# Own buffers and an interleaved order for a dense head's attention, passes dealt anew over the slots, hit matrices two to a slot, adjacency cast in place

## Chip, cores and metric

The kernel runs on one NeuronCore of a Trainium2 chip. The metric is the device time of one execution in microseconds, the median of repeated runs. The kernel before takes 17072.46 us (three runs, 17061.4 to 17086.94).

## What is computed

Sixteen graphs of 512 nodes with 128 features pass one layer made of two residual blocks:

```python
def gnn(x, adj):                      # x is layer-normed
    a = adj.astype(x.dtype)
    h = einsum('bnf,fu->bnu', x, W_msg)
    messages = einsum('bij,biu->bju', a, h) / sum(a, axis=1)      # mean over neighbours
    return relu(x @ W_upd + messages + bias)

def ffn(x):                           # x is layer-normed; 8 heads, 128 wide
    q = (x @ Wq) * 128 ** -0.5
    sim = einsum('pbnhd,pkhd->pbnhk', x @ Wq_pk, pk_keys)         # 2 sides of 128 keys
    # the 16 best of each side, the 16 best sums of 256 pairs, softmax of these:
    kv_scores, indices = product_keys(sim)
    k = einsum('bnhk,bnhkd->bnhd', kv_scores, keys_table[indices])
    v = einsum('bnhk,bnhkd->bnhd', kv_scores, values_table[indices])
    attn = softmax(where(causal, einsum('bihd,bjhd->bhij', q, k), -max))
    return einsum('bhij,bjhd->bhid', attn, v).reshape(b, n, 1024) @ Wo

x = x + gnn(layernorm(x), adj)
x = x + ffn(layernorm(x))
```

Each head has a table of 16384 rows of 256 numbers (key and value).

## The kernel before

The program goes over 16 batches (graphs). `batch` is written out for the first and the last one and is the body of a loop for the 14 between. Every engine has its own program, in an order that is fixed by hand; the engines meet at semaphores, and an engine whose next instruction waits does nothing else.

Seven of the eight heads are **gathered**. A batch has 28 **slots**; slot n is tile t = n % 4 (128 tokens) of head h = n // 4. For each slot POOL issues 16 indirect DMAs of table rows into one of three buffers `got` (L343). They need the row numbers (`rows_ready`) and the end of the slot that last read the buffer (`combined`). Row numbers come two tiles at a time: VectorE ranks the next head's scores in the four slots of a head and, at the end of slots t = 1 and t = 3, makes `lifted`; TensorE's `move` turns it into `score_ps`, and VectorE writes `rows` and `spread`. TensorE weighs the gathered rows (`comb_ps`, L580), ScalarE copies them to `kv`, and a chain of small steps does the tile's attention: `key_transpose`, `scores`, VectorE's `negate`, ScalarE's `exponent`, `prob_transpose`, `values`, `project`, VectorE's `add`.

The eighth head is **dense**: its whole table streams through `tab` (1 MB a chunk, SP's queue), and 128 **passes** a batch multiply it with weights that are worked out for every key. A pass is `raise_` (ScalarE, `expo`), `weigh` (VectorE, `wide`, L1114), `turn` (TensorE, four transposes, L456), a copy on ScalarE (`wideT`), and `multiply` (TensorE, L470). VectorE is one pass ahead of TensorE and can't run farther ahead (`wideT_ready`). Each slot has five places for passes, between the steps of its attention; the tuples `ONE`, `SIX` and `FEW` say how many stand at each place, and `MIDDLE` and `ENDING` say which tuple a slot has. Before, slots 1, 2, 15 and 16 have two passes and all others five.

The dense head needs, per batch, eight **hit matrices**: VectorE writes one (`hit`, 16 instructions, L1078), TensorE adds its 16 parts up (`add_hits`, L437), and VectorE takes the sum. They stand one in each of the slots 3 to 6 and 23 to 26.

The dense head's own attention has four tiles per batch. Two are done in slots 15 and 16 and two in slots 1 and 2 of the following batch (`OWN`, `LEFT`), each after the slot's gathered tile, with the same tensors `neg`, `prob`, `probT`, `headT` and the same parts of `score_ps` and `probT_ps`.

`front` (the next head's scores and queries) runs on TensorE ahead of the combine of a slot with t = 0, so its time counts to the slot before. The graph block of the next batch is spread over slots 8 to 20; the adjacency matrix is loaded as integers into `adj_i` and cast by ScalarE into `adj_f`.

## Time and profile before

| what | value |
|---|---|
| median time | 17072.46 us |
| span of the profiled execution, first to last instruction | 9595.0 us |
| time of the profiled execution beside its span | not recorded: the profile gives the span alone |
| median time less the span | 7477.5 us |
| TensorE busy (matmul) | 8080.2 us, 84% |
| VectorE busy | 7220.8 us, 75% |
| ScalarE busy | 4866.4 us, 51% |
| POOL busy, not counting the time between two issues | 6794.0 us, 71% |
| mean granted TensorE clock | 0.888 of 2.4 GHz |

The span has all 16 batches in it (7168 gathers, 448 slots of 16). What the device does outside of it, 44% of the time, leaves no instruction in the trace. No engine is full, and the shares are averages over slots that differ. A slot is read from one group of gathered matmuls (L580) to the next.

### The profile page before, as it was taken

The numbers are of one execution on the slowest core, as the hardware profiler recorded it, in microseconds if no ns is written. First come the engines' busy times: TensorE is split into PE (matmuls) and PEld (weight loads), VectorE is DVE, ScalarE is ACT, GpSimd is POOL, SyncE is SP. The second block draws the span as 40 slices with busy tenths as digits, with TensorE's granted clock in tenths as the row PEclk, the third lists the DMA queues.
The fourth block names the chain that finished last, engine by engine and source line by source line (L and its number), as shares of the span: only waits on it lengthen the run. The fifth ranks groups of instructions, "written<-read, shape, count | busy, mean of one in ns | idle before, by whom it ended". The sixth has DMA issues, their size and how long they took to land.

```text
span 9595.0 us, 181229 instructions
## 1 busy us (share of the span) xinstructions
PE 8080.2 (84%) x51232; PEld 6240.2 (65%) x51232; DVE 7220.8 (75%) x32005; ACT 4866.4 (51%) x14163; POOL 6794.0 (71%) x7177
## 2 busy tenths in 40 slices
PE   5888888888888888888888888888888888888898
PEld 4666666666666766667666676666666666666676
DVE  7787777877777777777776777777777777877775
ACT  3555445455454554545445454454554545545454
POOL 5777767777677776777767777677776767767666
PEclk7899889998888998889888898898998989988898
DMA  4555445554454554545444454455554545545454
GB/s 126 166 171 161 155 154 162 163 162 158 155 160 158 162 165 150 160 157 166 158 152 158 159 164 157 155 162 161 164 165 150 166 151 165 167 150 160 146 167 138
DMA packets 445985, 1516.88 MB, mean 158 GB/s; under 512 B 123760, under 2 KB 141552, under 8 KB 379248
## 3 DMA queue, kind: packets, MB, share of 16 engines
q0 software_dynamic: 344064, 939.98, 32.5%
q1 hardware_dynamic: 100848, 564.37, 16.8%
q8 instruction: 456, 7.47, 0.3%
q14 instruction: 617, 5.05, 0.2%
HBM read 1499.66 MB, written 4.19 MB: 157 GB/s over the span
## 4 chain that ended last, share of the span: by engine, by line
PE 53%; DVE 36%; issue 5%; ACT 5%; DVEq 1%; DMA 0%; ACTq 0%; SPq 0%
PE dense_ps L470 20%; DVE wide L1114 10%; PE comb_ps L580 10%; PE wideT_ps L456 5%; PE front_ps L410 4%; DVE onehot L1005 4%; PE score_ps L446 4%; DVE chosen L1010 3%; DVE hits L1078 3%; DVE onehot L998 3%; PE score_ps L507 2%; PE score_ps L495 2%; PE probT_ps L513 2%; DVE neg L1131 1%; ACT expo L706 1%
## 5 line engine op out<-in xcount | busy, mean ns | idle before, releaser
L343 POOL DMA_INDIRECT got<-in_table,rows x7168 | 6792.1, 948 | 2778.2 <-issue 2203.5
L470 PE MATMUL dense_ps<-tab,wideT 128*128 128x256 f32 x16384 | 3959.9, 385 | 4.7 <-ACT kv_d L641 3.8
L470 PEld LDWEIGHTS dense_ps<-tab,wideT 128*128 128x128 f32 x16384 | 3002.5, 192 | 640.4 <-issue 274.7
L1114 DVE SCALAR_TENSOR_TENSOR wide<-const_ps,rank,expo 128x128 f32<-128x128 f32 x8192 | 2303.7, 344 | 1268.0 <-PE wideT_ps L456 993.1
L706 ACT ACTIVATE expo<-sim_d,shift 128x128 f32<-128x128 f32 x8192 | 2596.8, 393 | 118.0 <-DVE wide L1114 117.3
L641 ACT ACTIVATE wideT<-wideT_ps 128x512 f32<-128x512 f32 x2048 | 1212.0, 592 | 1070.2 <-PE wideT_ps L456 1065.8
L456 PE MATMUL wideT_ps<-ident,wide 128*128 128x128 f32 x8192 | 1237.1, 274 | 118.3 <-DVE wide L1114 61.0
L456 PEld LDWEIGHTS wideT_ps<-ident,wide 128*128 128x128 f32 x8192 | 1005.9, 141 | 386.0 <-DVE wide L1114 101.6
L580 PE MATMUL comb_ps<-got,spread 128*32 128x256 f32 x14336 | 1078.7, 452 | 4.8 <-DVEq L1102 4.0
L446 PE MATMUL score_ps<-group_of,lifted 128*128 128x16 f32 x1792 | 344.1, 329 | 554.3 <-DVE lifted L1021 554.3
L580 PEld LDWEIGHTS comb_ps<-got,spread 128*32 128x32 f32 x14336 | 481.5, 126 | 491.3 <-issue 299.5
L446 PEld LDWEIGHTS score_ps<-group_of,lifted 128*128 128x128 f32 x1792 | 327.2, 273 | 591.9 <-DVE lifted L1021 565.4
L641 ACT ACTIVATE kv<-comb_ps 128x256 f32<-128x256 f32 x448 | 170.8, 381 | 878.1 <-PE comb_ps L580 876.7
L1078 DVE TENSOR_SCALAR hits<-iota_f,top_f_d,put 128x128 bf16<-128x128 f32 x2048 | 579.3, 357 | 0.6 <-DVE z_inv L1089 0.2
L746 ACT ACTIVATE prob<-neg,neg_max 128x128 f32<-128x128 f32 (+3 forms) x512 | 286.7, 560 | 518.9 <-DVE neg_max L1131 515.8
L641 ACT ACTIVATE sim<-front_ps 128x512 f32<-128x512 f32 x224 | 133.8, 597 | 819.8 <-PE front_ps L410 816.8
L501 PE MATMUL probT_ps<-ident,prob 128*128 128x128 f32 x1280 | 257.8, 304 | 300.3 <-ACT prob L746 300.3
L513 PE MATMUL probT_ps<-wo_sb,headT 128*128 128x128 f32 x1024 | 288.3, 369 | 187.8 <-ACT headT L641 187.8
L501 PEld LDWEIGHTS probT_ps<-ident,prob 128*128 128x128 f32 x1280 | 165.9, 153 | 394.4 <-ACT prob L746 394.4
L641 ACT ACTIVATE headT<-score_ps 128x128 f32<-128x128 f32 x512 | 141.8, 277 | 532.9 <-PE score_ps L507 532.9
L1005 DVE TENSOR_TENSOR onehot<-onehot,const_ps 128x1600 f32<-128x1600 f32 (+1 forms) x225 | 406.4, 1806 | 1.2
L998 DVE TENSOR_TENSOR onehot<-place,const_ps 128x1600 f32<-128x1600 uint32 (+1 forms) x225 | 406.8, 1808 | 0.0
(155 smaller groups left out, 8417.1 us busy)
## 6 DMA issues: line engine op xcount, KB each, us to landing
tab<-in_dense SPq DMA_DIRECT2D x512, 1024.0 KB
got<-in_table,rows POOLq DMA_INDIRECT x7168, 2.7
adj_i<-in_adj SPq DMA_DIRECT2D x16, 1024.0 KB, 9.6
x_in<-in_x SPq DMA_DIRECT2D x16, 256.0 KB
out<-fin SPq DMA_DIRECT2D x16, 256.0 KB, 6.0
tab<-in_wqpk_t SPq DMA_DIRECT2D x1, 512.0 KB, 11.0
tab<-in_keys_t SPq DMA_DIRECT2D x1, 512.0 KB, 15.5
wq_sb<-in_wq SPq DMA_DIRECT2D x1, 512.0 KB, 15.2
```

What stands on the lines that cost most here:

```text
L343: pool.indirect_dma_start(out=got[got_no(n)][:, g, :], out_offset=None, in_=table, in_offset=bass.IndirectOffsetOnAxis(ap=rows[:, t * GATH ...
L446: mm = pe.matmul(moved_ps[:, 2 * q + u, :], lifted[:, u, q, :, :].rearrange("p e r -> p (e r)"), group_of[:, :], start=True, stop=True)
L456: mm = pe.transpose(wideT_ps[:, q * P:(q + 1) * P], wide[k % 2][:, q, :], ident[:, :])
L470: mm = pe.matmul(dense_ps[:, v * 2 * D:(v + 1) * 2 * D], wideT[k % 2][:, (2 * u + v) * P:(2 * u + v + 1) * P], tab[(k // CHUNK) % 2][:, (2 ...
L513: pe.matmul(proj_ps, headT[:, :], wo_sb[:, h, :], start=True, stop=True).then_inc(projected, 1)
L580: mm = pe.matmul(comb_ps[j * BAND:(j + 1) * BAND, 0:2 * D], spread[:, t, g, :], got[got_no(n)][:, g, :], start=(c == 0), stop=(c == PER_BA ...
L641: return act.activation(dst, src, ACT.Copy, scale=scale)
L706: last = act.activation(expo[k % 2][:, 2 * u + v, :], sim_d[:, 2 * half + v, 0:NKEYS], ACT.Exp, bias=shift1[:, 2 * half + v, key:key + 1])
L998: after(link(dve.tensor_tensor(onehot[:, 0:nt, :, :].rearrange("p t k c -> p (t k) c"), place[:, t0:t0 + nt, :].rearrange("p t k -> p (t k ...
L1005: after(link(dve.tensor_tensor(hot, hot, cand_row[:, 0:nt, :].unsqueeze(2).broadcast_to([P, nt, TOPK, NCAND]), ALU.mult)))
L1078: last = dve.tensor_scalar(hits[:, a, :], iota_f[:, :], top_f_d[:, u, side, a:a + 1], put[:, u, side, a:a + 1], ALU.is_equal, ALU.mult)
L1114: last = dve.scalar_tensor_tensor(wide[k % 2][:, 2 * u + v, :], count_ps[:, v, :], rank1[:, 2 * half + v, key:key + 1], expo[k % 2][:, 2 * ...
```

## The change

The passes are dealt as 3 to 6 (in the last batch 3 to 7) a slot. The first slot of a head mostly has six, the fourth three or four. `THREE` and `FOUR` have no pass between `key_transpose` and `scores`, and `THREE` has none between `prob_transpose` and `values`. The last batch ends its passes with slot 23.

The dense head's attention has tensors of its own (`neg_d` to `headT_d`), the two banks of `front_ps` and its own semaphores. Each of its steps stands right behind the same step of the slot's gathered tile. Its own two tiles move from slots 15 and 16 to 17 and 18.

The hit matrices are made two to a slot, with two buffers, in slots 4, 8, 24 and 26. The adjacency matrix is cast onto itself, and its next load waits for the messages instead of the cast. The dense query moves from slot 3 to 5, and the graph block's matmuls are one slot earlier. Nothing is computed that was not computed before.

```diff
-ONE = (1, 1, 1, 1, 1)
+THREE = (1, 0, 1, 1, 0)
+FOUR = (1, 0, 1, 1, 1)
+FIVE = (1, 1, 1, 1, 1)
 SIX = (2, 1, 1, 1, 1)
-FEW = (1, 1, 0, 0, 0)
+SEVEN = (2, 1, 1, 2, 1)
-MIDDLE = [ONE] + [FEW] * 2 + [ONE] * 12 + [FEW] * 2 + [ONE] * 11
+MIDDLE = [
+    FIVE, FOUR, FOUR, THREE,
+    SIX, FOUR, FIVE, THREE,
...
-OWN = {15: 0, 16: 1}
+OWN = {17: 0, 18: 1}
 LEFT = {1: 2, 2: 3}
-OWN_LAST = {15: 0, 16: 1, 25: 2, 26: 3}
+OWN_LAST = {17: 0, 18: 1, 25: 2, 26: 3}
+HITS = {1: {4: (0, 1), 8: (2, 3)}, 0: {24: (0, 1), 26: (2, 3)}}
...
-    adj_f = sb("adj_f", [P, T, N])
+    adj_f = adj_i[:, :, :].bitcast(F32)
...
+    score_d_ps = front_ps[0]
+    headT_d_ps = front_ps[0][:, 0:P]
+    probT_d_ps = front_ps[1]
...
-                sp.wait_ge(adj_cast, b + 1)
+                sp.wait_ge(msg_ready, b * 2 + 2)
...
+        def key_transpose_dense(c, tile, f):
+
+            pe.wait_ge(kv_d_copied, c - tile + (tile // 2 * 2 + 2))
+            pe.wait_ge(q_copied, f)
+            pe.wait_ge(sim_copied, f * 2)
+            pe.wait_ge(added_d, c)
+            pe.transpose(keyT_d_ps, kv_d[:, tile, 0:D], ident[:, :]).then_inc(keyT_d_ready, 1)
...
+                values(slot, t)
                 if tile is not None:
...
+                    values_dense(c, tile)
+                project(slot, h)
+                if tile is not None:
+                    project_dense(c)
...
+                for g in sets:
+                    take_sum(of_d, half, g, sets[-1])
```

On TensorE, in slot 1 of a middle batch, this stood there before (tensors whose names end in `_d` are the dense head's; its attention here uses the common `score_ps` and `probT_ps`):

```order
L491 MATMUL probT_ps<-ident,kv 128x128
L470 MATMUL dense_ps<-tab,wideT 128x256 x4
...
L495 MATMUL score_ps<-keyT,qT 128x256
L501 MATMUL probT_ps<-ident,prob 128x128 x2
L507 MATMUL score_ps<-probT,kv 128x128 x2
L513 MATMUL probT_ps<-wo_sb,headT 128x128
...
L491 MATMUL probT_ps<-ident,kv_d 128x128
...
L495 MATMUL score_ps<-keyT_d,qT_d 128x384
L501 MATMUL probT_ps<-ident,prob 128x128 x3
L507 MATMUL score_ps<-probT,kv_d 128x128 x3
```

In the same slot of the changed kernel the order is this:

```order
L541 MATMUL probT_ps<-ident,kv 128x128
...
L571 MATMUL front_ps<-ident,kv_d 128x128
L545 MATMUL score_ps<-keyT,qT 128x256
...
L575 MATMUL front_ps<-keyT_d,qT_d 128x384
L520 MATMUL dense_ps<-tab,wideT 128x256 x4
...
L551 MATMUL probT_ps<-ident,prob 128x128 x2
L581 MATMUL front_ps<-ident,prob_d 128x128 x3
L520 MATMUL dense_ps<-tab,wideT 128x256 x4
...
L557 MATMUL score_ps<-probT,kv 128x128 x2
L587 MATMUL front_ps<-probT_d,kv_d 128x128 x3
L563 MATMUL probT_ps<-wo_sb,headT 128x128
```

Passes of the dense head now stand between the steps of both tiles, where before the second tile's steps followed one another with nothing between them.

On VectorE, in slot 4 of a middle batch, this stood there before (`wide` is a pass, `top_v` and `top_i` belong to the ranking):

```order
L1114 SCALAR_TENSOR_TENSOR wide<-const_ps,rank,expo 128x128 x4
L1078 TENSOR_SCALAR hits<-iota_f,top_f_d,put 128x128 x4
...
L939 MAX top_v<-sim 128x8 x4
L941 MAX_INDEX top_i<-top_v,sim 128x8 x4
...
L1114 SCALAR_TENSOR_TENSOR wide<-const_ps,rank,expo 128x128 x4
L1078 TENSOR_SCALAR hits<-iota_f,top_f_d,put 128x128 x4
L943 MATCH_REPLACE sim_rest<-top_v,sim 128x128 x4
```

In the changed kernel the same stretch reads so:

```order
L1211 SCALAR_TENSOR_TENSOR wide<-const_ps,rank,expo 128x128 x4
...
L1175 TENSOR_SCALAR hits<-iota_f,top_f_d,put 128x128 x4
...
L1034 MAX top_v<-sim 128x8 x4
L1036 MAX_INDEX top_i<-top_v,sim 128x8 x4
...
L1211 SCALAR_TENSOR_TENSOR wide<-const_ps,rank,expo 128x128 x4
L1175 TENSOR_SCALAR hits<-iota_f,top_f_d,put 128x128 x8
L1038 MATCH_REPLACE sim_rest<-top_v,sim 128x128 x4
```

The slot holds twice the hit instructions, and slots 3, 5, 6, 23 and 25 hold none.

## Rows read from the trace of the kernel before

**Rows 1.** Waits of POOL, whole run: total us, times, longest

```profile
POOL got L343 <- DVE rows L1029: 541.6, 123, 41.1
POOL got L343 <- PE comb_ps L580: 33.1, 20, 14.7
```

**Rows 2.** Timeline of POOL, first, middle, last: start, us, idle before

```profile
43.65 1.10 POOL L343 DMA_INDIRECT got<-in_table,rows  x1 [41.14 <-DVE rows L1029]
...
4800.49 0.95 POOL L343 DMA_INDIRECT got<-in_table,rows  x1 [0.30 <-issue]
...
9571.83 0.95 POOL L343 DMA_INDIRECT got<-in_table,rows  x1 [0.30 <-issue]
```

**Rows 3.** Windows: first, middle fourteen, last batch: us; busy PE PEld DVE ACT POOL; clock

```profile
115.90:675.96 560.06, 486.28 (x3154) 377.29 (x3153) 446.92 (x1988) 299.26 (x872) 410.23 (x433) 0.91 0.51 163
675.96:9000.60 8324.64, 7055.69 (x44801) 5452.17 (x44801) 6312.89 (x27960) 4256.78 (x12390) 5943.68 (x6274) 0.89 0.50 159
9000.60:9595.00 594.40, 501.86 (x3092) 381.60 (x3091) 381.89 (x1664) 293.26 (x867) 392.19 (x415) 0.88 0.47 148
```

**Rows 4.** Windows of one middle batch: its slots 1, 4, 5, 7, 8, 9, 11, 15, 23

```profile
4260.94:4287.97 27.03, 16.36 (x90) 11.54 (x90) 17.31 (x80) 8.38 (x27) 15.26 (x17) 0.69 0.38 123
...
4343.70:4359.29 15.59, 15.06 (x118) 12.49 (x118) 11.40 (x56) 11.25 (x35) 11.63 (x14) 1.00 0.51 161
4359.29:4382.88 23.59, 18.00 (x127) 14.68 (x127) 20.76 (x83) 11.55 (x36) 16.76 (x18) 0.95 0.50 157
...
4401.48:4425.43 23.95, 21.11 (x128) 16.35 (x128) 20.52 (x83) 11.54 (x34) 17.95 (x19) 0.93 0.59 193
4425.43:4439.84 14.41, 14.04 (x102) 11.53 (x101) 8.82 (x49) 10.92 (x34) 11.05 (x12) 1.00 0.47 141
4439.84:4458.98 19.14, 15.84 (x112) 12.90 (x111) 16.10 (x65) 14.11 (x40) 14.47 (x16) 1.00 0.57 190
...
4476.15:4499.41 23.26, 21.22 (x132) 16.24 (x132) 20.28 (x81) 12.14 (x35) 17.47 (x20) 0.94 0.60 196
...
4557.52:4589.18 31.66, 21.12 (x101) 14.84 (x100) 21.94 (x89) 7.91 (x24) 22.82 (x25) 0.68 0.43 134
...
4728.84:4757.10 28.26, 23.40 (x144) 18.11 (x143) 25.30 (x99) 11.77 (x34) 19.27 (x21) 0.88 0.46 141
```

**Rows 5.** Windows of the last batch: its slots 7 and 8

```profile
9172.91:9200.27 27.36, 25.11 (x140) 19.40 (x140) 19.86 (x76) 13.18 (x39) 17.25 (x19) 0.88 0.45 151
9200.27:9217.02 16.75, 16.38 (x113) 13.43 (x112) 10.38 (x55) 12.84 (x39) 12.79 (x14) 1.00 0.57 173
```

**Rows 6.** Waits of TensorE in that middle batch (4245.92 to 4843.14)

```profile
PE score_ps L446 <- DVE lifted L1021: 33.0, 12, 4.1
PE probT_ps L501 <- ACT prob L746: 18.8, 8, 5.7
PE probT_ps L513 <- ACT headT L641: 11.7, 32, 0.4
PE probT_ps L491 <- DVEq L1148: 7.1, 4, 4.3
PE score_ps L507 <- ACT probT L641: 4.2, 8, 0.7
```

**Rows 7.** Timeline of TensorE, slot 1 of that batch

```profile
4265.08 0.27 PE L491 MATMUL probT_ps<-ident,kv 128*128 128x128 f32 x1
...
4278.20 0.45 PE L491 MATMUL probT_ps<-ident,kv_d 128*128 128x128 f32 x1 [4.32 <-DVEq L1148]
```

**Rows 8.** Timeline of VectorE, slot 4 of that batch

```profile
4348.10 1.13 DVE L1114 SCALAR_TENSOR_TENSOR wide<-const_ps,rank,expo 128x128 f32<-128x128 f32 x4 [3.68 <-PE wideT_ps L456]
```

**Rows 9.** Waits of POOL in the first 660 us

```profile
POOL got L343 <- DVE rows L1029: 56.9, 8, 41.1
POOL got L343 <- PE comb_ps L580: 15.7, 2, 14.7
```

**Rows 10.** The cast of the adjacency: duration min/median/max in ns

```profile
L641 ACT ACTIVATE adj_f<-adj_i x16: 1899/1902/1909, 12.9 to 8666.7; 128x2048 f32<-128x2048 int32 x16
```

More of the change, by code:

```diff
@@ L81, in got_back, with dense_tile, fronts @@
     return next(d for d in range(1, 6) if got_no((n - d) % SLOTS) == got_no(n))
-def attend_no(b, n, left, first, last):
-    dense = set(OWN_LAST if last else OWN) | (set() if first else set(LEFT))
-    place = n + len([m for m in dense if m < n]) + left
-    return place if first else b * (SLOTS + T) + (place - 2)
+def dense_tile(b, n, first, last):
+    if n in (OWN_LAST if last else OWN):
+        return (OWN_LAST if last else OWN)[n], b
+    if n in LEFT and not first:
+        return LEFT[n], b - 1
+    return None, b
+def fronts(b, n, last):
+    return b * GH + (min(n // T + 2, GH) if last else n // T + 2)
 def program(nc, x, adj, w_msg, w_upd, bias, wqpk_t, keys_t, wq, table, dense, wo, out):
@@ L550, in batch @@
                     if h < GH - 1:
-                        front(b, h + 1, last)
+                        front(b, h + 1, first, last)
                     elif not last:
@@ L806, in batch @@
                 copy(kv[:, t, :], comb_ps[:, 0:2 * D]).then_inc(kv_copied, 1)
+                if n == 12 and not last:
+                    gnn_hu(b + 1)
                 k = passes(b, k, w[1], first, last)
-                take_keyT(a, t, keyT)
+                take_keyT(slot, t)
+                if tile is not None:
+                    take_keyT_dense(c, tile)
                 if n == 9 and not last:
@@ L814, in batch @@
                     gnn_adj(b + 1)
-                if n == 13 and not last:
-                    gnn_hu(b + 1)
                 if n == 17 and not last:
@@ L1197, in batch @@
                     half, of_d, o = 0, b + 1, n - PREP[0]
+                sets = HITS[1].get(n, ()) if half == 1 else HITS[0].get(n, ()) if half == 0 else ()
                 def hit_part(part):
-                    if half is not None and 3 <= o <= 6:
-                        hit(of_d, half, o - 3, part)
-                a = attend_no(b, n, 0, first, last)
+                    for g in sets:
+                        hit(of_d, half, g, part)
+                tile, of = dense_tile(b, n, first, last)
+                c = of * 4 + (tile or 0)
                 k = passes(b, k, w[0], last)
@@ L1227, in batch @@
                     gnn_in(b + 1)
-                if n == 15 and not last:
+                if n == 14 and not last:
                     gnn_msg(b + 1)
```

229 lines of the change are left out of this document (150 added, 79 removed).

## The prediction

> **What bounds the kernel now.** I read the waits of POOL first, because POOL looks idle for 29% of the span and is not. One gather takes 0.95 us and the next one starts 0.30 us behind it [rows 2]. From the first gather at 43.65 to the last at 9571.83 there are 7167 steps. Less the waits in between, 574.7 - 41.1 = 533.6 us [rows 1], that is (9528.2 - 533.6) / 7167 = 1.255 us a gather, 20.1 us a slot, and 562.2 us a batch of 28 slots. A middle batch takes 8324.64 / 14 = 594.6 us [rows 3]. So the gathers alone would need 95% of the time, and POOL can be handed 32 us a batch back at the very most.
>
> The other 32 us are POOL's waits for row numbers. Those come out of a loop between TensorE and VectorE, and that loop sets the pace of a middle batch. In the windows of one middle batch the reader is to see two kinds of slot. In slot 4 TensorE is busy for 15.06 of 15.59 us: TensorE is the limit. In slot 5 it is busy for 18.00 of 23.59 us and VectorE for 20.76: VectorE is the limit, and TensorE waits ahead of `move` [rows 4]. Over the batch the waits of TensorE name the two stalls: 33.0 us for `lifted` at the end of odd slots, and the steps of the dense tile's attention [rows 6]. Slots 1 and 15, which have only two passes, still last 27.0 and 31.7 us, at a granted clock of 0.69 and 0.68 [rows 4]; slots 2 and 16 are of the same kind.
>
> I therefore cost two chains per batch, the TensorE-VectorE loop (594.6 now) and the gathers (562.2, unchanged), and ask which is longer afterwards.
>
> **The dense tile's attention, four tiles a batch.** It stands alone in its slots, so each wait between its steps is bare. Going are 18.8 us ahead of the probabilities' transposes, 7.1 ahead of the key's transpose, 4.2 ahead of the values, and four of the 32 waits ahead of the projection, 4 x 0.37 [rows 6]: together 31.6 us. The 7.1 are the shared buffers: the dense tile can't begin before the gathered tile is added. Behind those waits `move` is queued, and POOL waits for its rows. The steps' own time stays, since the same matmuls are done. A stall can return if no pass covers it; slots 1, 17 and 18 have a pass or two between each pair of steps except key and scores. Bounds: 24.5 go if the 7.1 stay because VectorE is late for its own reasons in slot 1 (17.31 busy of 27.03), 31.6 go at best. I take 31.6.
>
> **The clock in these slots.** One transpose takes 0.27 us in slot 1 while the clock is up and 0.45 us behind the 4.32 us wait [rows 7], 1.6 times as long. At a mean of 0.68, 64% of slot 15 is at 1.2 GHz, the lower of the two levels, so of its 21.12 us of TensorE work 0.64 x 21.12 x (1 - 1/1.6) = 5.1 us are lost, and by the same sum 3.8 in slot 1. With slots 2 and 16 some 16 us a batch at most. The passes that move into these slots are then done at the higher clock, but slots 1 and 15 wait for VectorE as well. Bounds 0 and 16, I take 6.
>
> **Hit matrices.** A slot with one costs more than its like without one: slot 5 against slot 9 is 23.59 - 19.14 = 4.45, slot 23 against 11 is 5.0, slot 4 against 8 is 1.2 [rows 4]. They are dear where VectorE is the limit. Leaving are slots 3 and 23 (5.0 each), 5 and 25 (4.45 each), and 6 (I take the 1.2 of slot 4): 20.1 us. Coming are a first one in slot 8 (1.2) and a second one in 4, 8, 24 and 26. VectorE has a gap of 3.68 us in slot 4, waiting for TensorE's front and combine [rows 8], and the second matrix lies partly in it; each costs between 1.2 and 4.45. Coming in all: 6.0 to 19.0. Net -14.1 to -1.1, I take -8.
>
> **Passes.** They stay 128. By the new plan the first slots of the seven heads have 41 (32 before), the second 31 (32), the third 33 (32), the fourth 23 (32). Nine passes go from fourth slots to first ones. The last batch has one pass more per slot than a middle one at slots 7 and 8, which prices a pass: 27.36 - 23.95 = 3.4 in a fourth slot, 16.75 - 14.41 = 2.3 in a first [rows 4, 5]. By these rows the move gives 9 x (2.3 - 3.4) = -9.9. If instead VectorE alone holds the fourth slot, taking a pass away gives back just its 1.13 us there [rows 8], and the move costs 9 x (2.3 - 1.13) = +10.5. Between ends of both signs I take 0.
>
> **Holes.** Where a tuple has no pass between two steps, TensorE waits for ScalarE's copy, 0.4 us as ahead of the projection, 11.7 / 32 [rows 6]. Thirteen slots lack the second place, and five of them the fifth as well: 18 x 0.4 = +7. It is 0 if `lifted` is late anyway, since TensorE then waits the same time twice over. I take 7.
>
> **Edits at nothing.** The cast is one instruction of 1.9 us a batch in either form [rows 10]. Its next load now waits for messages of slot 13 of the batch before, long past when SP comes to it; without that cover SP's queue would hold up the table's chunks. The dense query and the graph block's matmuls move by a slot or two with the same instructions. The new waits on `added_d` in `front` are for tiles two or more slots back. The extra buffers cost nothing.
>
> **Sum.** Loop: 594.6 - 31.6 - 6 - 8 + 0 + 7 = 556.0 us a batch. Gathers: 562.2. They have come within about 1% of each other, and neither is even, so they will trip over each other now and then: rows come in pairs, POOL is at most three buffers ahead, and TensorE now meets gathers that have not landed. The first batch is such a case already: without left dense tiles it takes 560.1 us [rows 3], and POOL waits 72.6 - 41.1 = 31.5 us in it [rows 9], most of it in its start-up. I add 5 us to the longer chain: 567 a batch. That is 27.6 us less in each of 14 middle batches (386), 25 in the last one, which has the same stalls, and 0 in the first. In all 411 of the 502 us that POOL waits behind the first 660 us (574.7 - 72.6) [rows 1, 9]. Span 9595.0 - 411 = 9184.
>
> The median is 17072.5, 7477.5 above the span, and the trace has nothing of that part. I take it as unchanged: same inputs, same outputs. **17072.5 - 411 = 16,661 us.**
>
> **Rivals.**
>
> *The gathers become the only bound* (0.20). If the low ends hold, the loop falls to 594.6 - 31.6 - 16 - 14.1 - 9.9 = 523, TensorE waits for gathers in every slot, and all 502 us go: 16,570 us. For it: the first batch's 560 with two dense tiles still serial. Against it: 523 needs four low ends at once.
>
> *Half of it is given back* (0.20). With the high ends, 594.6 - 24.5 - 0 - 1.1 + 10.5 + 7 = 586.5, the loop stays the bound, and the change gives 8.1 x 15 = 122, 16,950 us. Midway between 556 and 586.5 it is 571, and the change gives 23.6 x 14 = 330, 16,740 us. The case is what lies between. For it: fourth slots where VectorE is busy for 20.3 of 23.3 us (slot 11). Against it: the price of a pass in slot 7.
>
> *Nothing comes of it* (0.05): the dense steps wait for each other in the new order too, since ScalarE and VectorE take both tiles in turn; 17,040 to 17,100.
>
> *The clock falls, and it is slower* (0.07). Stalls that were collected in four slots are now holes in all of them, beside waits for gathers, and TensorE is granted less everywhere. The mean in a middle batch is 0.89 [rows 3]; if all slots went to the 0.69 of slot 1, the half-speed share would go from 0.22 to 0.62, and 504 us of TensorE work would grow by about 0.40 x 504 x 0.375 = 76 us, to a loop of 556 + 76 = 632: 37.4 x 15 = 561 us slower, 17,630 us. It decides from a mean of about 0.79, where the growth eats the 38.6 us that the loop gained. Against it: slots 4 and 8, with the densest TensorE work, stand at 1.00, and passes are put into the starved slots. The Trainium skill ("TensorE: Matmul & The Clock Gate", The HAM clock gate) says that the default is the throttled state and that activity releases it. By that rule more and shorter waits speak against this change; the trace agrees so far that the clock is low where TensorE sits idle (0.69 at 16.36 busy of 27.03).
>
> **How the numbers follow.** The forecast (16,600 to 16,740) has 0.48. A measurement here tells changes from 0.2% on, 34 us. Faster than that: 0.48 + 0.20 + 0.19 of the third case = 0.87; same 0.05; slower 0.08 (the clock 0.07, the rest 0.01). The range runs from the gathers' floor with some room, 16,550, to 16,890, which takes in the better half of the third case and leaves out about 0.18.
>
> **What the profile will show.** Right: POOL's waits for rows fall from 541.6 to below 200 us; a middle batch takes 562 to 570; slots 1, 2, 17, 18 last about 20 to 22 us at a clock above 0.85; the waits ahead of the dense tile's transposes are gone; waits of `comb_ps` for gathers appear. The hit slots 4, 8, 24, 26 last 18 to 22 us, and slots 5 and 25 under 20. Wrong: a middle batch above 580 us with `lifted` as TensorE's largest wait and more than 33 us of it; a clock below 0.85; a gather step above 1.26 us; or a span that falls while the time does not, which would mean that the part outside the span is not fixed.

## The result, and the profile after

The changed kernel takes 16523.39 us (median of four runs, 16515.62 to 16534.99), and beside it the kernel before takes 17066.93 (four runs, 17061.18 to 17086.94). The ratio is 0.968, with a 95% interval of 0.9666 to 0.9694: 543.5 us less, where 411 were forecast. The time lies 27 us below the range.

The span of the profiled execution is 16533.2 us, 1.8 us below its own time of 16534.99. So almost nothing lies outside the span. The prediction had 7477.5 us there, worked out from a span and the times of other executions, and took them as fixed. The trace of before that is shown ahead comes from an execution in which signals between engines came on time; in every other traced execution of before or after with all its gathers back to back they came late.

From the page of the kernel after, its span, its engines and the chain that ended last:

```profile
span 16533.2 us, 180655 instructions
## 1 busy us (share of the span) xinstructions
PE 8989.4 (54%) x51232; PEld 6835.3 (41%) x51232; DVE 7249.1 (44%) x32005; ACT 4856.2 (29%) x14163; POOL 6787.8 (41%) x7177
...
another core or an unknown queue 40%; DVE 22%; PE 21%; issue 10%; ACT 6%; DVEq 0%; ACTq 0%; DMA 0%; SPq 0%
```

No engine is busy for more than 54%, and 40% of the chain has no releaser in this trace, on a kernel with one core. Windows of its first batch, its middle fourteen and its last one (span of the window, busy time of each engine, clock, DMA share, GB/s), to set against [rows 3]:

```profile
147.21:1160.28 1013.07, 548.09 (x3154) 417.99 (x3153) 449.91 (x1993) 298.73 (x872) 412.20 (x436) 0.74 0.28 90
1160.28:15563.28 14403.00, 7875.30 (x44802) 5986.98 (x44801) 6339.16 (x27972) 4248.27 (x12390) 5937.58 (x6272) 0.75 0.29 92
15563.28:16533.18 969.90, 530.27 (x3092) 401.80 (x3091) 379.71 (x1652) 292.11 (x867) 390.40 (x413) 0.75 0.29 91
```

A middle batch lasts 14403.00 / 14 = 1028.8 us. The busy time of VectorE, ScalarE and POOL is what it was in [rows 3]; the engines do the same work and stand still for longer. Windows of slots 1 to 6 of one middle batch, against [rows 4]:

```profile
7385.96:7406.82 20.86, 16.73 (x115) 13.54 (x114) 18.89 (x86) 11.36 (x37) 0.00 (x0) 0.95 0.15 51
7406.82:7462.41 55.59, 22.88 (x113) 16.09 (x112) 15.33 (x80) 9.73 (x29) 30.26 (x32) 0.65 0.30 95
7462.41:7485.89 23.48, 19.07 (x104) 13.82 (x103) 17.39 (x67) 8.12 (x24) 2.18 (x3) 0.80 0.21 63
7485.89:7540.08 54.19, 25.64 (x147) 19.23 (x146) 19.82 (x90) 12.29 (x37) 28.05 (x30) 0.68 0.36 114
7540.08:7556.39 16.31, 13.75 (x101) 11.10 (x100) 14.70 (x60) 10.74 (x33) 0.00 (x0) 1.00 0.19 67
7556.39:7608.53 52.14, 19.64 (x107) 15.25 (x106) 12.20 (x57) 9.40 (x28) 30.26 (x32) 0.67 0.33 101
```

The reader is to see that slots take turns. Where POOL issues 30 or 32 gathers, which are the gathers of two slots in one go, the slot lasts 52 to 56 us. Where it issues none to three, it lasts 16 to 23 us, as in [rows 4]. This goes on up to slot 23; slots 24 to 27 share out their gathers and last 32 to 37 us each in the mean of the middle batches. The waits of POOL over the whole run, against [rows 1]:

```profile
POOL got L388 <- DVE rows L1124: 6681.7, 210, 44.5
POOL got L388 <- issue: 2349.5, 6879, 30.1
POOL got L388 <- PE comb_ps L661: 585.2, 31, 32.0
```

POOL waits twelve times as long for `rows` as in [rows 1]. These are not the stalls of before: gathers and loop take turns. The largest waits of the other engines (total us, times, longest) say why:

```profile
DVE wide L1211 <- remote: 6089.0, 464, 42.4
PEld wideT_ps L506 <- issue: 6003.2, 676, 34.1
ACT wideT L722 <- remote: 5165.6, 403, 37.2
PE wideT_ps L506 <- ACT wideT L722: 3395.7, 315, 33.8
```

"remote" is a wait whose end the trace can put down to none of this core's engines, since the instruction waited for had long been done. One of them, step by step. First TensorE in one slot, 8004.81 to 8059.64:

```profile
8014.50 1.89 PE L520 MATMUL dense_ps<-tab,wideT 128*128 128x256 f32 x8
8024.28 1.09 PE L506 MATMUL wideT_ps<-ident,wide 128*128 128x128 f32 x4 [7.89 <-issue]
8025.16 3.62 PE L520 MATMUL dense_ps<-tab,wideT 128*128 128x256 f32 x8
8052.35 1.09 PE L506 MATMUL wideT_ps<-ident,wide 128*128 128x128 f32 x4 [23.57 <-ACT wideT L722]
```

ScalarE and VectorE in the same stretch:

```profile
8023.54 0.60 ACT L722 ACTIVATE wideT<-wideT_ps 128x512 f32<-128x512 f32 x1 [9.62 <-remote]
...
8051.61 0.60 ACT L722 ACTIVATE wideT<-wideT_ps 128x512 f32<-128x512 f32 x1 [18.40 <-remote]
```

```profile
8023.61 1.13 DVE L1211 SCALAR_TENSOR_TENSOR wide<-const_ps,rank,expo 128x128 f32<-128x128 f32 x4 [10.54 <-remote]
...
8051.69 1.13 DVE L1211 SCALAR_TENSOR_TENSOR wide<-const_ps,rank,expo 128x128 f32<-128x128 f32 x4 [16.26 <-remote]
```

And POOL:

```profile
8045.34 0.95 POOL L388 DMA_INDIRECT got<-in_table,rows  x1 [0.30 <-issue]
8078.50 0.94 POOL L388 DMA_INDIRECT got<-in_table,rows  x1 [32.21 <-DVE rows L1124]
```

POOL gathers in steps of 1.25 us up to 8045.34. While it does, TensorE's four transposes of 8024.28 end at 8025.4, and ScalarE, which copies what they made and has been idle for 18.40 us, starts at 8051.61, 26 us later and 5 us behind the end of POOL's last gather. TensorE then waits for that copy, VectorE for TensorE. POOL is silent until 8078.50, and the next slot, from 8059.64 on, goes at its normal pace (25.16 us). The trace also records when each signal takes effect. The listing has the median distance from the end of an instruction to the next recorded signal on its semaphore ("gathering" is an instruction that starts less than 1.6 us behind the start of a gather). Some signals are missing from the records, 93 of `dense_ps`'s 2048 in after, so medians are read and not the longest ones:

```
                                  POOL silent    POOL gathering
after, TensorE's dense_ps           0.014 us         9.4 us
after, TensorE's wideT_ps           0.014 us        10.6 us
after, ScalarE's wideT              0.009 us        13.0 us
before, the trace shown ahead,
        TensorE's dense_ps             -             0.014 us
```

So signals of TensorE and ScalarE arrive some 10 us late while POOL issues gathers back to back. VectorE's `wide` is on time in the median in the same stretches (0.011 us).

The Trainium skill ("Perfetto Trace Analysis", Summary: the profiler window per engine type) lists the propagation of a semaphore as hidden from the profiled windows of TensorE, VectorE and ScalarE. This trace agrees: VectorE and ScalarE are busy for 7249.1 and 4856.2 us, against 7220.8 and 4866.4 in the trace shown ahead, and the lateness shows only in idle time and, here, in the events of the semaphores. (TensorE is busy for 8989.4 us instead of 8080.2, at a granted clock of 0.745 instead of 0.888.)

The Trainium skill ("Perfetto Trace Analysis", Identifying the Most-Contended Engine) also judges VectorE, ScalarE and GpSimd (POOL) by occupancy, the share of time in which they execute, and says to optimize the engine with the highest first; of TensorE it takes the share of the peak arithmetic rate and the busy share of the weight loads instead. By the busy shares VectorE would come first here (44%), and POOL, whose gathers the next section shows to be the cause, stands at 41%, no higher than the weight loads.

### The profile page after: what moved, and what is told of

The parts are those of the page before. It is cut to its first block, busy times and chain, and to the rows that moved or that the text cites. A ratio compares the mean times of both kernels' runs of the same rounds, so it can differ in the third digit from the quotient of the medians.

```text
span 16533.2 us, 180655 instructions
## 1 busy us (share of the span) xinstructions
PE 8989.4 (54%) x51232; PEld 6835.3 (41%) x51232; DVE 7249.1 (44%) x32005; ACT 4856.2 (29%) x14163; POOL 6787.8 (41%) x7177
## 4 chain that ended last, share of the span: by engine, by line
another core or an unknown queue 40%; DVE 22%; PE 21%; issue 10%; ACT 6%; DVEq 0%; ACTq 0%; DMA 0%; SPq 0%
PE dense_ps L520 8%; DVE wide L1211 6%; PE comb_ps L661 3%; ACT expo L787 3%; PE wideT_ps L506 2%; DVE hits L1175 2%; DVE onehot L1100 2%; PE score_ps L496 2%; DVE onehot L1093 2%; DVE chosen L1105 1%; PE front_ps L460 1%; ACT wideT L722 1%; PE score_ps L557 1%; DVE lifted L1116 1%
## 5 line engine op out<-in xcount | busy, mean ns | idle before, releaser
L388 POOL DMA_INDIRECT got<-in_table,rows x7168 | 6785.8, 947 | 9720.1 <-DVE rows L1124 6681.7
L506 PE MATMUL wideT_ps<-ident,wide 128*128 128x128 f32 x8192 | 1477.8, 310 | 5993.1 <-ACT wideT L722 3395.7
L520 PE MATMUL dense_ps<-tab,wideT 128*128 128x256 f32 x16384 | 4572.7, 427 | 115.9 <-issue 99.4
L520 PEld LDWEIGHTS dense_ps<-tab,wideT 128*128 128x128 f32 x16384 | 3423.6, 219 | 935.6 <-issue 413.0
L545 PE MATMUL score_ps<-keyT,qT 128*128 128x512 f32 (+3 forms) x896 | 390.3, 523 | 244.3 <-issue 144.9
L557 PE MATMUL score_ps<-probT,kv 128*128 128x128 f32 x2240 | 366.2, 299 | 207.3 <-ACT probT L722 197.1
L722 ACT ACTIVATE probT<-probT_ps 128x128 f32<-128x128 f32 x448 | 194.4, 434 | 926.7 <-remote 689.5
L827 ACT ACTIVATE prob<-neg,neg_max 128x128 f32<-128x128 f32 x448 | 251.0, 560 | 696.2 <-DVE neg_max L1228 452.8
L1248 DVE SCALAR_TENSOR_TENSOR acc<-probT_ps,prob_inv,acc 128x128 f32<-128x128 f32 x414 | 145.3, 351 | 661.0 <-PE probT_ps L563 614.2
L557 PEld LDWEIGHTS score_ps<-probT,kv 128*128 128x128 f32 x2240 | 316.7, 210 | 227.0 <-ACT probT L722 215.9
L1105 DVE TENSOR_REDUCE chosen<-onehot 128x32 f32<-128x1600 f32 (+1 forms) x225 | 406.1, 1805 | 2.8
```

The lines of the kernel that those rows point to most:

```text
L388: pool.indirect_dma_start(out=got[got_no(n)][:, g, :], out_offset=None, in_=table, in_offset=bass.IndirectOffsetOnAxis(ap=rows[:, t * GATH ...
L506: mm = pe.transpose(wideT_ps[:, q * P:(q + 1) * P], wide[k % 2][:, q, :], ident[:, :])
L520: mm = pe.matmul(dense_ps[:, v * 2 * D:(v + 1) * 2 * D], wideT[k % 2][:, (2 * u + v) * P:(2 * u + v + 1) * P], tab[(k // CHUNK) % 2][:, (2 ...
L557: last = pe.matmul(headT_ps, kv[:, j, D:2 * D], probT[:, j * P:(j + 1) * P], start=(j == 0), stop=(j == t))
L722: return act.activation(dst, src, ACT.Copy, scale=scale)
L1105: link(dve.tensor_reduce(chosen[:, 0:nt, 0, :], onehot[:, 0:nt, :, :], AX.X, ALU.add))
```

## The experiments

Times differ from chip to chip and, on one chip, from one hour to another: the kernel before took 17067 us beside the changed kernel, and 17231, 17098, 17275, 17251, 17224 and 17259 us beside the kernels of this section, in their order; 17275 and 17224 are of one chip. So differences of tens of us are taken within one group, and across groups by the ratio to before.

**Two theories.** A: the time is in the span, the loop is slowed by late signals, and the trace shown ahead lacked them. B, the prediction's: something fixed lies outside the span. The first kernel is before, unchanged.

> The kernel before, unchanged, for a second trace. The changed kernel's trace has a span as long as its time (16,533 us), and in it signals of TensorE and ScalarE reach their waiters 10 us late in the median while POOL issues gathers, and 0.01 us late when it does not. The first trace of the kernel before had none of that and a span 7,477 us short of its median. Theory A (that trace caught an execution in a rare undisturbed condition; the timed ones have late signals too): the new span is 17,050 to 17,090 us, slots last about 20 us without gathers and 45 us or more with them, and a middle batch takes about 1,060 us. Theory B (the kernel's executions really span 9,600 us and some 7,470 us lie outside the instructions): the new span is 9,590 to 9,600 us again.

Its time is 17236.39 us and its span 17234.6. From the page, the middle fourteen batches, and the waits of POOL:

```profile
span 17234.6 us, 181229 instructions
...
PE 9315.1 (54%) x51232; PEld 6957.4 (40%) x51232; DVE 7244.2 (42%) x32005; ACT 4886.6 (28%) x14163; POOL 6781.2 (39%) x7177
```

```profile
1180.63:16195.62 15014.99, 8148.41 (x44801) 6085.19 (x44801) 6333.35 (x27965) 4275.29 (x12390) 5930.84 (x6271) 0.72 0.29 88
```

```profile
POOL got L343 <- DVE rows L1029: 7344.9, 209, 49.4
POOL got L343 <- issue: 2386.7, 6860, 34.3
POOL got L343 <- PE comb_ps L580: 536.7, 32, 33.4
```

B is gone: in every execution of before or after whose span is on record, timed or traced, span and time are less than 2 us apart. Of the trace shown ahead the own time isn't on record, so its 9595.0 us stood beside the times of other executions. A middle batch of before takes 15014.99 / 14 = 1072.5 us, not 594.6, and its waits for `rows` are 7344.9 us, not the 541.6 of [rows 1]. Signals are late here too: 6.7 us for `dense_ps` and 10.0 for `wideT_ps` and `wideT` in the median, measured as above.

**Are the gathers the cause?** Before and after with one gather a slot; the other fifteen are left out, and zeros stand in their place:

```diff
+KEEP = (0,)
...
-                for c in range(PER_BAND):
-                    for g in range(c, GATHERS, PER_BAND):
+                for g in KEEP:
```

> The kernel before with one gather a slot instead of 16; the other 15 parts of got hold zeros, so the attention of the seven gathered heads is computed from wrong keys and values with the same instructions. Theory (gathers hold back the signals of the other engines): the late signals are gone, and the span is that of the TensorE-VectorE loop alone, 594.6 us a middle batch as in the undisturbed trace of before, 9,550 to 9,650 us in all. Rival (this condition of the chip delays signals whatever POOL does): the span stays above 13,000 us.

> The changed kernel with one gather a slot instead of 16, zeros in the rest of got (wrong keys and values in the gathered heads, the same instructions). It measures the loop that the prediction put at 556 us a middle batch. If the prediction's sum for the loop is right, 552 to 560 us a middle batch and a span of about 8,950 us; if the gain of 544 us lies wholly in the loop, 594.6 - 36 = 558 or less. If the loop is shorter by less than 25 us, most of the gain comes from how the work falls into the times with and without gathers.

9549.14 and 9184.22 us. Middle batches, before and then after:

```profile
686.69:8959.80 8273.11, 7013.12 (x44801) 5417.40 (x44800) 6296.73 (x27960) 4255.54 (x12390) 371.26 (x392) 0.90 0.20 67
```

```profile
676.38:8653.90 7977.52, 6926.38 (x44801) 5399.10 (x44800) 6286.10 (x27972) 4240.05 (x12390) 370.57 (x392) 0.93 0.21 69
```

That is 590.9 and 569.8 us a batch; for after 552 to 560 were expected. Before with one gather a slot runs as the trace shown ahead did with sixteen (594.6), and its signals are on time (0.014 us for `dense_ps`). So the lost time hangs on the gathers, and the loop itself got 21.1 us a batch shorter, 365 us in all. What TensorE still waits for in after:

```profile
PE score_ps L501 <- DVE lifted L1121: 540.7, 224, 15.9
PE wideT_ps L511 <- ACT wideT L727: 258.5, 139, 4.4
PE probT_ps L568 <- ACT headT L727: 140.9, 384, 0.4
PE score_ps L550 <- ACT keyT L727: 78.8, 220, 0.7
```

`lifted` stays at 541 us (554.0 with before's gathers cut down so), the projection's 187.8 fell to 140.9, the 299.5 ahead of the probabilities' transposes are gone, and 258.5 for ScalarE's `wideT` have come (51.8 before).

**Number, bytes or both?** `KEEP` of eight gathers, and all sixteen with half the bytes of each row:

```diff
-                            out=got[got_no(n)][:, g, :], out_offset=None, in_=table,
+                            out=got[got_no(n)][:, g, 0:D], out_offset=None, in_=table,
...
-        "table": c(table[:GH * ROWS]),
+        "table": c(table[:GH * ROWS]).reshape(-1, D),
```

> The changed kernel with eight gathers a slot instead of 16, zeros in the rest of got (wrong keys and values in the gathered heads). If the time that is lost goes with the time in which POOL issues gathers, half of them take 3584 x 1.25 = 4,480 us less of such time, and the span lies near the middle between 16,533 us and the span with one gather a slot, 12,500 to 13,200 us. If POOL's rate of issue were to blame only where it has no pause, the span falls nearly to that of one gather.

> The changed kernel with all 7168 gathers, each of half the bytes (128 numbers a row instead of 256, from a table cut in half rows; wrong keys and values, zeros for the rest). If the number of gathers and their completion signals delay the other engines' signals, the span stays within 300 us of 16,533. If the bytes moved do it, the span falls by a third or more of what half as many gathers give.

11600.01 and 16504.47 us. Half the bytes leave the time where it was: 16504 / 17098 = 0.965 of before, against after's 0.961 to 0.968. The loss per gather is (16533 - 9184) / 6720 = 1.09 us with sixteen a slot and (11600 - 9184) / 3136 = 0.77 us with eight: it is their number, and more than in proportion. For eight gathers 12,500 to 13,200 us were expected, in proportion; 11,600 is below that. The signals of `dense_ps` are 3.3 us late with eight gathers and 8.9 us with half the bytes.

**The parts of the change**, each undone by itself in the kernel after: after again, the hit matrices back at one a slot, the old deal of passes, and the dense tile's steps put one behind the other.

```diff
-HITS = {1: {4: (0, 1), 8: (2, 3)}, 0: {24: (0, 1), 26: (2, 3)}}
+HITS = {1: {3: (0,), 4: (1,), 5: (2,), 6: (3,)}, 0: {23: (0,), 24: (1,), 25: (2,), 26: (3,)}}
```

```diff
+FEW = (1, 1, 0, 0, 0)
+MIDDLE = [FIVE] + [FEW] * 2 + [FIVE] * 14 + [FEW] * 2 + [FIVE] * 9
...
```

```diff
                 project(slot, h)
                 if tile is not None:
+                    if n in LEFT:
+                        pe.wait_ge(sim_d_copied, b * 2 + 2)
+                    key_transpose_dense(c, tile, fronts(b, n, last))
+                    if tile == 0:
+                        pe.wait_ge(q_d_copied, b + 1)
+                    scores_dense(c, tile)
+                    prob_transpose_dense(c, tile)
+                    values_dense(c, tile)
                     project_dense(c)
...
```

> The changed kernel, unchanged, beside the next three on the same chip. It should take 0.968 of the time of the kernel before, some 545 us less.

> The changed kernel with the hit matrices one to a slot in slots 3 to 6 and 23 to 26, as before. With one gather a slot the change shortens the loop by 365 us, with 16 by 545. Theory A (the hit matrices filled VectorE in slots that it limited): this is 60 to 200 us slower than the changed kernel. Theory B (they now lie in first and third slots, where VectorE waits for late signals anyway, so they cost nothing there): also slower, and by the whole price in the second and fourth slots, 20.1 - 2.4 us a batch, about 280 us. If it is within 35 us, the hit matrices play no part.

> The changed kernel with the passes dealt as before: five a slot (six in the last batch), two in slots 1, 2, 17 and 18, where the dense tiles are. The prediction put the deal at 0 and its holes at 7 us a batch, so by it this is 0 to 105 us faster. Rival: in the changed kernel's trace the first and third slots hold the gathers and last 46 to 56 us, the second and fourth 17 to 25; a pass in a slot with gathers costs several waits for late signals, so moving nine passes from fourth to first slots costs time too, and this is over 100 us faster. Other rival: the fourth slots are the ones without gathers, where each pass costs 2.3 us or more and is gone from the path, while the gathers' time passes anyway; then this is 150 to 350 us slower.

> The changed kernel with the dense head's attention behind the gathered tile's, step after step with no pass between, in its own buffers and in slots 1, 2, 17, 18. The bare waits come back, 24.5 us a batch without the waits for shared buffers, so this is 300 to 400 us slower than the changed kernel by the undisturbed rows. If late signals make each of the dense tile's eight hand-overs dear when gathers run (slots 2 and 18 have gathers), it is more than 400 us slower.

| kernel | us | ratio to before [95%] | above after |
|---|---|---|---|
| after | 16599.59 | 0.9609 [0.9593, 0.9625] | |
| hits apart | 16638.9 | 0.9631 [0.9615, 0.9647] | 39 |
| old deal | 16623.67 | 0.9623 [0.9607, 0.9639] | 24 |
| dense steps in a row | 16980.06 | 0.9831 [0.9815, 0.9847] | 380 |

ScalarE and VectorE do their parts of the dense tile in that order too. The interleaving is most of what the three give, 380 us where 300 to 400 were expected. The intervals of the other two overlap with that of after. Each of their runs is longer than the longest of after's four (16534.04 to 16603.7), so both cost something when undone, but no more than some 40 us each, and neither expectation was met: 60 us or more for the hit matrices, and for the deal a kernel that is faster, or slower by 150 us or more. All three undone at once, and the serial version with one gather a slot:

> The changed kernel with three parts undone together: dense attention serial, passes dealt as before, hit matrices one a slot. Apart they cost 380, 24 and 39 us. What is left of the change is own buffers, dense tiles in slots 17 and 18 instead of 15 and 16, the graph block a slot earlier and the cast in place. If the parts add up, it is 443 us slower than the changed kernel and some 230 us faster than before. If the parts depend on each other (hit matrices and the deal fill the same idle time of VectorE), it comes within 100 us of before.

> The serial order of the dense attention with own buffers, one gather a slot and zeros in the rest of got (wrong keys and values in the gathered heads). With 16 gathers the serial order cost 380 us against the interleaved one. If that is the bare waits of the loop, it costs the same here, 9,184 + 330 to 400 us. If a part of it comes from late signals, it costs less here, under 300 us.

Three undone: 17064.22 us, ratio 0.9893 [0.9877, 0.991]. That is 0.0284 above after's 0.9609, and the parts give 0.0022 + 0.0014 + 0.0222 = 0.0258, so they about add up (some 230 us faster than before were expected); it is still 187 us faster than before. What is left of the change in it are the own buffers, the other two slots of the dense tiles, the graph block a slot earlier and the cast in place. Its trace against the second trace of before says where: in the mean of the middle batches slots 14 to 18 are 12.5 us shorter together, slots 1 and 2 are 5.2 shorter, slots 12 and 13 are 5.2 longer, and the whole batch is 9.8 shorter. The serial version with one gather a slot takes 9524.73 us, 340 above after with one gather: the steps cost 22.7 us a batch when signals are on time and 25.3 when they are late. These two ran on different chips, but their slots 12, 13 and 20 to 27, where the edit does nothing, last the same within 0.2 us.

**What makes the signals late?** Theory B1: gathers back to back pile something up that other engines' signals wait behind, and a pause lets them out. Theory B2: each gather holds the loop up for its 1.09 us, whatever stands between two. A pause is a fill of `idle` on POOL and a wait for it:

```diff
                         ).then_inc(gathered_end[c] if last and n == SLOTS - 1 else gathered[t], 16)
...
+                        pool.memset(idle[:, :], 0.0).then_inc(paced, 1)
+                        pool.wait_ge(paced, slot * GATHERS + turn)
...
```

> The changed kernel, all gathers, but POOL clears a spare tile of 512 columns (0.53 us in the trace) after each gather and waits for it, so gathers start some 2 us apart instead of 1.25. Theory A (the loop stands still in proportion to the number of gathers, about 1.09 us for each): no gain, 16,400 to 16,700 us. Theory B (signals pile up only where gathers follow each other without a pause): the pauses let them through, a slot takes at most 16 x 2 = 32 us, and the span falls to 14,500 to 15,500 us.

> As the last one with 1024 columns, gathers some 2.5 us apart: POOL alone needs 7168 x 2.5 = 17,900 us. Theory A: POOL is the bound and the loop is held up in it, 18,000 us or more. Theory B: also about 18,000 us, POOL's own time, but with signals that are hardly late; the median delay of TensorE's signals in stretches of gathers falls from some 9 us to under 1 us.

16940.06 and 19984.90 us, the first above what either theory was expected to give, the second above the 18,000 that was expected of POOL alone. The POOL of the first:

```profile
8000.67 0.95 POOL L390 DMA_INDIRECT got<-in_table,rows  x1 [0.81 <-POOL idle L396]
8001.62 0.54 POOL L396 MEMSET idle<- 128x512 f32 x1
8002.97 1.44 POOL L390 DMA_INDIRECT got<-in_table,rows  x1 [0.81 <-POOL idle L396]
```

A fill and the wait for it cost more than was taken: gathers stand 2.34 and 2.76 us apart, where some 2 and 2.5 were expected. The slots last 37.7 and 44.5 us in the mean of the middle batches, which is sixteen such steps, and the median lateness of TensorE's signals is back at 0.014 us while POOL gathers. By its time alone the first of the two fits B2 as well (20.4 + 16 x 1.09 = 37.8 us a slot); the signals on time, the even slots and the second kernel speak for B1, with POOL as the bound and the loop beside it. The two theories part on shorter and rarer pauses, which by B1 are faster than both kernels: a 128x16 fill after each gather, the 128x512 fill after every second one, and after every fourth one, this last in before too.

> As the kernel after, but GpSimd sets 128x16 values to zero after each gather and waits for that before it issues the next: a pause a good deal shorter than the 128x512 one (0.54 us of work, gathers 2.34 us apart, 16,940 us). All gathers and all results are kept. Pauses let the signals through: the delays stay near zero as with the long pause, gathers stand some 1.9 us apart (2.34 less some 0.45 of the shorter fill), GpSimd is the bound at 16 x 1.9 = 30.4 us a slot, and 448 x 30.4 = 13,600 us. Rival, what counts is the number of gathers whatever stands between them unless the pause is long: a slot takes the loop's 20.4 us and 16 x 1.09 = 17.4 us more, 37.8 us or some 16,700 us.

> As the kernel after, with the 128x512 fill and its wait after every second gather instead of every one. All results are kept. Pauses let the signals through, and two gathers in a row do not yet pile anything up: GpSimd takes 8 x (2 x 1.25 + 1.1) = 28.8 us a slot, 12,900 us. Rival, only a pause behind each gather keeps the signals on time: signals late by several us again inside each pair, slots of 35 us and more, over 15,500 us.

> As the kernel after, with the 128x512 fill and its wait after every fourth gather. All results are kept. Pauses let the signals through, and four gathers in a row are few enough: GpSimd takes 4 x (4 x 1.25 + 1.1) = 24.4 us a slot, 10,950 us, with signals late by up to some 5 us inside a run of four, so 11,000 to 13,000 us. Rival, the delay grows with the gathers in a row and the loop stands for most of each run: as the kernel with eight gathers a slot lost 0.77 us for each gather, 20.4 + 16 x 0.77 = 32.7 us a slot, 14,700 us or more.

> The kernel before with the same fill and wait after every fourth gather. All results are kept. If GpSimd's 24.4 us a slot are the bound here too, it ends within 100 us of the kernel after paced so, and the change is worth next to nothing; if signals are late and the loop sets the end, it is 365 us (the gain measured with one gather a slot) or more above it.

13958.7, 13069.35, **11204.54** and 11203.8 us. Expected by B1 were 13,600, 12,900 and 11,000 to 13,000 us, by its rivals some 16,700, over 15,500 and 14,700 or more, so B2 is out. The third has a ratio of 0.6505 [0.6494, 0.6516] to before, with the same gathers and the same result plus 1792 fills. POOL in it (start, us, idle before):

```profile
8018.31 0.54 POOL L397 MEMSET idle<- 128x512 f32 x1
8019.66 0.95 POOL L390 DMA_INDIRECT got<-in_table,rows  x1 [0.81 <-issue]
8020.91 0.94 POOL L390 DMA_INDIRECT got<-in_table,rows  x1 [0.30 <-issue]
8022.16 0.94 POOL L390 DMA_INDIRECT got<-in_table,rows  x1 [0.30 <-issue]
8023.41 0.94 POOL L390 DMA_INDIRECT got<-in_table,rows  x1 [0.30 <-issue]
8024.34 0.55 POOL L397 MEMSET idle<- 128x512 f32 x1
```

Its waits of POOL and the first of TensorE:

```profile
POOL got L390 <- DVE rows L1131: 55.9, 6, 40.8
...
PE comb_ps L668 <- DMA got<-in_table,rows: 1147.7, 322, 11.0
```

Four gathers and a pause take 6.1 us. POOL waits 55.9 us for rows in the whole run, 6681.7 without pauses, and TensorE waits for gathers instead. The prediction's picture of two chains side by side holds in this kernel, and the gathers are the longer one. Before and after paced so end within 1 us of each other: **with POOL as the bound the change is worth nothing measurable**, though its loop is 21 us a batch shorter. The last run took the short pause after every fourth gather:

> As the kernel after, with the short fill (128x16) and its wait after every fourth gather. All results are kept. The short pause behind each gather put two gathers 1.92 us apart instead of 1.25, the long one 2.34. If a pause works by being there, GpSimd takes 4 x (3 x 1.25 + 1.92) = 22.7 us a slot, and 448 x 22.7 = 10,160 us, with up to some 200 us more where a slot of the loop is longer than that: 10,150 to 10,400 us. Rival, four gathers in a row need the longer pause to let the late signals out: the loop falls behind and the time is above the 11,204 us of the long pause.

14627.64 us, ratio 0.8472 [0.8458, 0.8486], where 10,150 to 10,400 were expected: the rival. Its POOL:

```profile
8014.19 0.95 POOL L390 DMA_INDIRECT got<-in_table,rows  x1 [0.30 <-issue]
8015.45 0.95 POOL L390 DMA_INDIRECT got<-in_table,rows  x1 [0.30 <-issue]
8016.40 0.13 POOL L397 MEMSET idle<- 128x16 f32 x1
8036.50 0.95 POOL L390 DMA_INDIRECT got<-in_table,rows  x1 [19.98 <-DVE rows L1131]
```

POOL waits for rows again, and a median signal of `dense_ps` is 2.9 us late. The runs side by side, "a gather" being POOL's step with its share of the pause:

| kernel | us a gather | sixteen | slot, middle batches | lateness of `dense_ps` |
|---|---|---|---|---|
| after | 1.25 | 20.0 | 36.7 | 9.4 us |
| short fill, every 4th | 1.42 | 22.7 | 32.6 | 2.9 |
| 128x512, every 4th | 1.52 | 24.4 | 24.9 | 0.47 |
| 128x512, every 2nd | 1.80 | 28.8 | 29.1 | 0.014 |
| short fill, each | 1.92 | 30.7 | 31.0 | 0.015 |
| 128x512, each | 2.34 | 37.4 | 37.7 | 0.014 |

From 1.52 us a gather upwards a slot lasts what POOL needs; at 1.42 the loop is held up. In the table the mean pace orders the lateness, and a short pause is enough where it stands behind each gather. But pace, length of the pause and number of gathers in a row were not changed apart: the short pause behind every fourth gather is shorter than the long one and gives a faster pace as well, and at the same 1.25 us eight gathers a slot gave 3.3 us where sixteen gave 9.4. What the signals wait behind, the gathers' own traffic or something else that comes with their issue, is not shown.

## Why the prediction was wrong

**The step that failed** is "The median is 17072.5, 7477.5 above the span, and the trace has nothing of that part. I take it as unchanged". The part was in the span of every execution whose span is on record, as waits of all engines (17234.6 against 17236.39 us in the second run of before). The last of the prediction's signs of being wrong doubts that the part is fixed, and yet it got no chance and no width: 44% of the time stood in the sum with a bound of zero on both sides. What ruled there is not the longer of loop and gathers but nearly their sum: before, 590.9 + 562.2 = 1153.1 us a batch, of which 80.6 overlap to give the 1072.5 measured; after, 569.8 + 562.2 = 1132.0, of which 103.2 overlap to give 1028.8. So the two chains "within about 1% of each other" never stood side by side, and the rival "the gathers become the only bound" came about only with pauses. The signs that the prediction named as right failed with it: POOL waits 6681.7 us for rows instead of less than 200, and a middle batch takes 1028.8 us instead of 562 to 570.

**That the sum came near** (411 against 543) is luck. The loop's gain was over-estimated, 38.6 us a batch against 21.1 with one gather a slot. With late signals the change gave another 178 us (543 - 365) that the sum didn't have.

**The dense tile's attention**, 31.6 with bounds from 24.5. The serial version costs 22.7 us a batch with signals on time, near the low bound without the 7.1 of the buffers; this term was right in kind. The waits ahead of the probabilities' transposes, 299.5 us, are gone with one gather a slot as said, and so are the 114.3 us (7.1 a batch) for the shared buffers.

**Buffers, clock, hit matrices and holes**, -7.1 - 6 - 8 + 7 = -14.1 us a batch, measured together (365 - 340) / 15 = -1.7 with one gather a slot (passes and the other dense slots in it); a middle batch of the serial version takes 590.3 us, before's 590.9. The waits for the buffers are gone in it, so other edits cost what that gave. One that is on record: with one gather a slot TensorE waits 258.5 us for `wideT` in after and 235.6 in the serial version, 51.8 before, some 12 us a batch that no term of the sum had; which edit brought them was not tried. Ahead of the scores, where the holes are, the waits for `keyT` and `keyT_d` went from 25.5 to 78.8 us, 3.3 a batch. The hit slots are the part that was off most visibly: with one gather slots 4, 8, 24 and 26 last 24.2, 25.6, 24.0 and 20.4 us (15.6, 14.4, 15.5 and 18.5 before, with fewer passes in the first three), where 18 to 22 were forecast. These four cost 30.2 us more, with the passes that came there, and slots 3, 5, 6, 23 and 25 gave back 25.6; slots 5 and 25, at 17.1 and 18.9, are under 20 as forecast. Slots 4 and 8 of after with one gather a slot:

```profile
4173.84:4198.05 24.21, 21.05 (x148) 16.65 (x147) 18.98 (x89) 12.41 (x37) 0.94 (x1) 0.93 0.27 93
...
4252.38:4277.97 25.59, 19.90 (x145) 16.31 (x145) 20.34 (x97) 13.95 (x42) 0.95 (x1) 0.93 0.14 47
```

TensorE's work in slot 4 went from 15.06 us [rows 4] to 21.05. Timed by itself, with late signals, the placing is worth 39 us or 2.6 a batch, a third of the 8 taken, at a size near the spread of these runs.

**Passes**: 0 was taken between ends of both signs, and 24 us or 1.6 a batch is what they gave, which those runs hardly tell from nothing.

**The clock**: 0.745 in the profile, which by the prediction's own mark (below 0.85) would be the fourth rival. It isn't: before stands at 0.724 in the same condition, and with one gather it goes from 0.895 to 0.923, up by the change both times. Slots 1, 2, 17 and 18 then last 21.1, 18.0, 17.8 and 16.7 us, where 20 to 22 were forecast.

**Left open**: why the traced execution of before that is shown ahead had its signals on time, with gathers 1.255 us apart; by what path gathers hold up signals; and by which of the remaining edits the 187 us come (own buffers, moved dense tiles, graph block, cast), of which one gather a slot shows only some 25. The shorter slots 14 to 18 point at the moved dense tiles, and fewer exchanges of signals inside the gathering stretch would explain it; no run tells.

## What to carry to other kernels

Compare the span with the time of its own execution before anything is worked out from a trace; in all runs here they are 2 us apart, and the trace whose own time was missing was of another condition. Its rows described the loop well (594.6 us against 590.9 with one gather a slot) and said nothing of what made up the other 44%. Where no engine is full and the largest waits are "remote", look at what one engine issues in long runs, and try a pause in it: here 1792 fills of 0.54 us on POOL took 17224 us to 11204, and an order of work that had been polished for the loop became worth nothing measurable. While loop and gathers took turns, an edit that shortened the loop alone by 365 us gave 543; once POOL was the bound, it gave nothing.

## What the runs showed of the hardware

While POOL issued indirect gathers 1.25 us apart, signals of TensorE and ScalarE took effect 9 to 13 us late in the median in the trace of after (7 to 10 us in the second one of before), against 0.009 to 0.014 us with POOL silent; those of VectorE's `wide` were on time in the median (0.011 us). In one trace of before, with gathers at the same 1.25 us, all were on time in the median. The lost time depended on the number of gathers (0.77 us each for eight, 1.09 for sixteen) and not on their bytes (16504 us at half the bytes, on a chip where before takes 17098; 16523 in full where it takes 17067). At a mean of 1.52 us a gather and above, by pauses of POOL, the loop kept up with POOL; at 1.42 it did not. Granted clock and stalls went together: 0.745 at 54% busy, 0.923 with one gather at 86%.
